# First attention of a two-layer gated cross-attention block: 64 unrolled slots, with probabilities and queries turned by VectorE and DMA

## The reference

```python
xn = layernorm(x);  q = xn @ Wq;  k = ctx @ Wk;  v = ctx @ Wv        # per head: 128 x 128
q = q * rsqrt(mean(q*q) + eps) * gq;  k = k * rsqrt(mean(k*k) + eps) * gk
p = softmax(q @ k.T / sqrt(128));  x = x + tanh(g_xattn[0]) * ((p @ v) @ Wo)
```

## Time and profile before

| What | Value |
|---|---|
| Median of 3 runs | 1292.04 us (1291.64 to 1292.76) |
| Profiled execution | 1293.64 us, span 1291.9 us, mean granted TensorE clock 0.992 |
| PE busy | 1238.0 us (96% of the span), 7907 matmuls |
| PEld busy | 1096.8 us (85%) |
| DVE busy | 893.5 us (69%), 2453 instructions |
| ACT busy | 737.3 us (57%), 2053 instructions |
| POOL busy | 550.6 us (43%), 542 instructions |
| DMA | 101.09 MB, mean 78 GB/s |

### The profile page before, as it was taken

One profiled execution on the slowest core, in us unless ns is written; L12 is line 12 of the kernel. 1 busy time (PEld: TensorE's weight loads), 2 busy tenths in 40 slices (PEclk: granted clock), 3 DMA queues, 4 the chain that ended last, 5 costly groups with the idle time before them and its releaser, 6 DMA issues. The chain is left out here.

```text
span 1291.9 us, 23370 instructions
## 1 busy us (share of the span) xinstructions
PE 1238.0 (96%) x7907; PEld 1096.8 (85%) x7907; DVE 893.5 (69%) x2453; ACT 737.3 (57%) x2053; POOL 550.6 (43%) x542
## 2 busy tenths in 40 slices
PE   6899999999999989999999989999999998999998
PEld 4788888888888878888888889898898987888987
DVE  6678788887988767743433235757777688788857
ACT  4877777777777744332222237766656554546542
POOL 4565456545566433200000001766667778223430
PEclk9999999999999989999999989999999999999999
DMA  8000000000000220299100000434334447413434
GB/s 268 10 1 1 9 1 1 1 9 0 0 0 1 65 41 2 64 331 293 65 0 1 1 18 17 152 120 123 115 107 142 124 126 251 119 46 101 131 100 174
DMA packets 85672, 101.09 MB, mean 78 GB/s; under 512 B 16985, under 2 KB 72802, under 8 KB 85186
## 3 DMA queue, kind: packets, MB, share of 16 engines
q1 hardware_dynamic: 82162, 90.45, 23.1%
q0 software_dynamic: 3408, 9.34, 2.0%
HBM read 53.60 MB, written 46.18 MB: 77 GB/s over the span
## 5 line engine op out<-in xcount | busy, mean ns | idle before, releaser
L98 PE MATMUL bank<-wvo_hi,pc_hi_a 128*128 128x256 f32 x512 | 148.8, 291 | 5.8 <-DVE pc_lo_a L1346 5.0
L1755 ACT ACTIVATE act_g_f<-bank 128x512 f32<-128x512 f32 x64 | 38.2, 598 | 191.1 <-PE bank L100 191.1
L100 PE MATMUL bank<-wvo_hi,pc_lo_a 128*128 128x256 f32 x512 | 143.8, 281 | 0.0
L99 PE MATMUL bank<-wvo_lo,pc_hi_a 128*128 128x256 f32 x512 | 143.7, 281 | 0.0
L1814 DVE TENSOR_TENSOR hid_f<-act_g_f,bank 128x512 f32<-128x512 f32 x64 | 44.0, 687 | 142.4 <-ACT act_g_f L1755 142.4
L883 ACT ACTIVATE probs_a<-bank,nbias_a,q_r_a 128x128 f32<-128x128 f32 x256 | 114.3, 472 | 23.6 <-DVE nbias_a L1001 23.4
L140 POOL TENSOR_TENSOR rstd<-mv,half 128x4 f32<-128x4 f32 x12 | 12.2, 1019 | 260.9 <-DVE mv L135 260.9
L1061 POOL TENSOR_TENSOR probs_a<-probs_a,rden_a 128x512 f32<-128x512 f32 x64 | 66.6, 1041 | 104.7 <-DVE rden_a L1007 104.7
L98 PEld LDWEIGHTS bank<-wvo_hi,pc_hi_a 128*128 128x128 f32 x512 | 97.4, 190 | 12.0 <-DVE pc_lo_a L1346 7.7
L1286 ACT ACTIVATE probs_a<-probs_a,nmin_a 128x128 f32<-128x128 f32 x256 | 99.6, 392 | 5.7 <-DVE nmin_a L1330 5.3
L98 PE MATMUL bank<-xt_hi_f,w_gu_hi_f 128*128 128x512 f32 (+1 forms) x256 | 101.2, 395 | 0.0
(11 more groups left out here) (314 smaller groups left out, 4138.7 us busy)
## 6 DMA issues: line engine op xcount, KB each, us to landing
rows_in<-blank_f SPq DMA_DIRECT2D x8, 2193.0 KB, 20.6
staged<-blocks_a SPq DMA_DIRECT2D x32, 512.0 KB, 2.9
turned_a<-staged SPq DMA_DIRECT2D x128, 128.0 KB, 3.0
xs_raw_f<-rows_in SPq DMA_DIRECT2D x39, 129.0 KB
y_tok_f<-rows_out SPq DMA_DIRECT2D x4, 1024.0 KB, 9.0
we_raw<-in_L_ffn_We_gate_up SPq DMA_DIRECT2D x2, 1408.0 KB, 9.6
ctx_raw_a<-in_ctx SPq DMA_DIRECT2D x8, 256.0 KB, 2.9
x_sb<-in_x SPq DMA_DIRECT2D x4, 512.0 KB, 9.9
```

The costliest lines, as they stand in the source:

```text
L98: nc.tensor.matmul(out, w[0], x[0], start=start, stop=False)
L99: nc.tensor.matmul(out, w[0], x[1], start=False, stop=False)
L100: return nc.tensor.matmul(out, w[1], x[0], start=False, stop=stop)
```

## The change

The first attention gets a function of its own, `first_attention`, and a flat order, `first_order`. The loop, the start, first, body and last parts and `quad_order` go. A slot v (from -7 to 71) holds one step of every kind, each for a unit that is some slots ahead or behind: for example Q of unit v+7, K of v+6, KT of v+3, S of v+2, EX of v+1, C of v-6 and W of v-7.

- T and QT leave TensorE. TV (VectorE) turns the probabilities of a unit in blocks, and TQ (VectorE) turns the queries straight out of the bank, in place of the copy Qv. SP swaps the blocks through DRAM for two units at a time, once for queries and once for probabilities. Qc (ScalarE) copies the landed queries, Th (ScalarE) the landed probabilities. Tl moves from VectorE to GpSimd.
- The powers of queries and keys become one GpSimd instruction for two units, RT, 16 values per row, once in two slots. Eps is added by a 129th column of the squares, so the two small VectorE additions go.
- The ring has three banks in place of two. `Kr` and `Qr` stay on VectorE, `KH` and `Rp` on GpSimd.
- The packed weights are loaded in parts: the first four tiles in slots 53 to 55, the scales in slot 57, the rest after slot 64. SC waits for the scales, CO of tile 0 for the first part and CO of tile 4 for the rest. The fed steps get new places by slot.

```diff
-FEED = {"Sm3": "SC0", "Tl1": "CO0", "Cl1": "LNB0", "Rp3": "VA0", "Tl3": "X0 X1", "Cl3": "CO1 VA1 DG0 DD0", "W0'": "CO2 VA2", "W1'": "DG1 DD1"}
+FEED = {55: "SC0", 56: "CO0", 57: "LNB0 VA0", 58: "X0 X1", 59: "CO1 VA1", 60: "DG0 DD0 CO2", 61: "VA2", 62: "DG1 DD1"}
...
+def first_order():
+    opening = """
+        WK0 CT0 CT1 LNA0 K0 Kc0 Kq0 K1 Kc1 Kr0 Kq1 LNB0 K2 Kc2 Kr1 Kq2 WQ0 K3 Kc3 Kr2 Kq3 X0 X1 Kr3 GN0"""
+    lead = {-7: "WK1", -6: "WQ1", -5: "VT0 VT1", -4: "VT2 VT3 CN0", -3: "VO0", -2: "WK2 VO1", -1: "WQ2 VO2", 0: "VO3", 1: "WK3 VO4", 2: "WQ3 VO5", 3: "VO6", 4: "VO7"}
+    norm = {0: "LA0", 1: "LA1", 2: "LA2", 3: "LA3", 4: "LM0", 5: "LB0", 6: "LB1", 7: "LB2", 8: "LB3 CT0", 10: "CT1"}
...
+    for v in range(-7, U + LAG):
+        s = v + 2 - LAG
+        if 0 <= v < U - H and v % H == 9:
+            words("X0 X1", v // H + 1)
+        unit(v + 2, "S")
+        unit(v + 6, "TQ", "Qq")
+        unit(v, "R", "Rp")
+        if v < U:
+            unit(v - 1, "TV")
+        unit(v + 3, "KT")
+        unit(v + 2, "Sm")
+        unit(v + 1, "EX")
+        unit(s, "C")
+        if v + 6 > 3:
+            unit(v + 6, "K")
+        if v + 5 > 3:
+            unit(v + 5, "Kr")
+        unit(v + 6, "Qr")
+        if v % 2 == 0:
+            unit(v + 4, "RT")
+        unit(v + 4, "KH")
+        words(lead.get(v, ""))
+        unit(s - 1, "W")
...
+        unit(s, "Ch", "Cl")
...
+        unit(v + 3, "KTc", "Qc")
+        if v + 6 > 3:
+            unit(v + 6, "Kc", "Kq")
+        unit(s + 1, "Th", "Tl")
+        unit(v + 7, "Q")
...
+            def swap(p, made, source, via, sent, target, landed, free, taken):
+                s = p % 2
+                sp.wait_ge(sem(made), 2 * p + 2)
+                if p >= 2:
+                    sp.wait_ge(sem(f"{landed}{s}"), 64 * (p // 2))
+                sp.dma_start(via[s], source[:, s, :, :, :].rearrange("p j u x -> p (j u x)")).then_inc(sem(sent), 16)
+                if p >= 2:
+                    sp.wait_ge(sem(free), taken)
+                sp.wait_ge(sem(sent), 16 * (p + 1))
+                rows = via[s].rearrange("(i r) (j x) -> j r i x", i=4, j=4)
+                for j in range(4):
+                    sp.dma_start(target[32 * j:32 * j + 32, s, :, :, :].rearrange("p i u x -> p i (u x)"), rows[j]).then_inc(sem(f"{landed}{s}"), 16)
...
+            for v in range(-5, U + 1):
+                if v % 2:
+                    p = (v + 5) // 2
+                    if p < U // 2:
+                        swap(p, "q_blocks_made", q_blocks, staged[1], "q_blocks_sent", q_turned, "q_landed", "q_copied", 2 * p - 2)
+                elif v >= 2:
+                    p = (v - 2) // 2
+                    swap(p, "blocks_made", blocks, staged[0], "blocks_sent", turned, "landed", "pt_ready", 2 * p - 2)
...
                 elif name == "KT":
+                    pe.wait_ge(sem("kh_ready"), n + 1)
...
+                elif name == "C":
...
+                    pe.wait_ge(sem("pt_ready"), n + 1)
+                    if n:
+                        pe.wait_ge(sem("pc_ready"), n)
...
+                elif name == "Qc":
+                    act.wait_ge(sem(f"q_landed{n // 2 % 2}"), 64 * (n // 4 + 1))
...
+                elif name == "TQ":
+                    dve.wait_ge(filled["Q"], n + 1)
...
+                    nc.vector.transpose(q_blocks[:, p % 2, :, n % 2, :].rearrange("p j (h t) -> p h j t", h=QH),
+                                        bank[:, :].rearrange("p (h j s) -> p h j s", h=QH, j=4)).then_inc(sem("q_blocks_made"), 1)
...
+                elif name in ("Kr", "Qr"):
...
+                    nc.vector.tensor_reduce(sums_of(kind, n), squares[:, n % 2, :, :], AX.X, ALU.add).then_inc(sem(f"{low}_summed"), 1)
...
+                elif name == "RT":
+                    pool.wait_ge(sem("q_summed"), n + 2)
+                    pool.wait_ge(sem("k_summed"), n + 2)
...
+                    nc.gpsimd.tensor_tensor(roots[:, p % 4, :, :, :].rearrange("p k u h -> p (k u h)"), ss[:, p % 2, :, :, :].rearrange("p k u h -> p (k u h)"),
+                                            core.half[:, :], ALU.pow).then_inc(sem("roots_ready"), 1)
                 elif name == "KH":
+                    pool.wait_ge(sem("roots_ready"), p + 1)
...
+                elif name == "Tl":
+                    pool.wait_ge(sem("pt_hi_ready"), n + 1)
+                    hi, lo = (v[:, n % 2, :].rearrange("p (i x) -> p i x", i=4) for v in pt)
+                    nc.gpsimd.tensor_tensor(lo, turned[:, n // 2 % 2, :, n % 2, :], f32(hi), ALU.subtract).then_inc(sem("pt_ready"), 1)
```

More of the change, by code:

```diff
@@ L441 @@
 PREPARE = ("UV", "UK", "UC", "UO", "UQ", "UM", "MB")
[L442 to L480, removed]
@@ L483, in with_weights @@
[L483 to L495, removed]
+FIRST_RING = ("X", "CT", "K", "Q", "KT", "VT", "VO")
+RING = ("X", "Q", "SR", "NX", "RT", "RK", "XF")
+DRAINED = {"Qc": "Q", "RL": "RT", "PL": "RK"}
@@ L496, in attention, with first_attention @@
+def first_attention(nc, core, block, w, a, norm, norm_after, packed, feed):
     ctx_dram = a["ctx_1024"]
@@ L522, in attention @@
[L522 to L533, removed]
-            q_r = sb("q_r", [P, 2, GB, QH])
-        else:
-            cm = sb("cm", [P, GB, P])
-            scores = probs
@@ L588, in walk @@
-        def walk(emit):
-            if L == 0:
-                for s in orders["start"]:
-                    emit("start", -1, *s)
-                for s in orders["first"]:
-                    emit("first", 0, *s)
-                with emit.engine.Fori(1, G - 1) as g:
-                    for s in orders["body"]:
-                        emit("body", g, *s)
-                for s in orders["last"]:
-                    emit("last", G - 1, *s)
-            else:
-                for g, *s in flat_order:
-                    emit("flat", g, *s)
@@ L663, in _ @@
+            for t in range(4, NF0 // P, 4):
+                for m in range(3):
+                    packed.load_words(sp, m, t)
+            feed.rest["sync"](sp)
         @block.tensor
         def _(pe):
[L665 to L685 removed]
@@ L687, in _, with bank_free @@
-            fed = feed.steps["tensor"](pe) if feed else None
-            def step(part, g, name, i, j):
-                m = round_of(name, g, j)
+            fed = feed.steps["tensor"](pe)
+            def bank_free(step):
+                at = ring.index(step)
+                if at >= 3:
+                    old = ring[at - 3]
+                    pe.wait_ge(sem({"Q": "q_squared", "K": "k_copied", "KT": "kt_copied", "X": "x_split", "CT": "ct_split", "VT": "vt_copied",
+                                    "VO": "vo_split"}[old[0]]), count(*old))
+                return ring_bank[at % 3]
@@ L907, in _ @@
+                    if n:
+                        act.wait_ge(sem("c_filled"), n * H)
+                    nc.scalar.activation(flat(cn[0][:, :, :]), flat(ctx_raw[:, :, :]), ACT.Copy).then_inc(sem("cn_hi_ready"), 1)
+            feed.rest["scalar"](act)
         @block.vector
         def _(dve):
-            fed = feed.steps["vector"](dve) if feed else None
-            def step(part, g, name, i, j):
-                m = round_of(name, g, j)
+            fed = feed.steps["vector"](dve)
+            for name, n, i in order:
+                bank = bank_of(name, n, i)
+                p = n // 2
@@ L1036, in _ @@
-            if feed:
-                feed.rest["vector"](dve)
+            feed.rest["vector"](dve)
         @block.gpsimd
         def _(pool):
-            fed = feed.steps["gpsimd"](pool) if feed else None
-            def step(part, g, name, i, j):
-                m = round_of(name, g, j)
+            fed = feed.steps["gpsimd"](pool)
+            nc.gpsimd.memset(core.ident[:, :], 0.0).then_inc(sem("zeroed"), 1)
+            nc.gpsimd.memset(core.half[:, :], -0.5).then_inc(sem("half_made"), 1)
@@ L1433, in flamingo @@
                     with nc.Block() as block:
-                        attention(nc, core, block, layer, w, a, gate_up, norm, norm_ffn, packed, router, None, feed)
+                        first_attention(nc, core, block, w, a, norm, norm_ffn, packed, feed)
                 else:
```

736 lines of the change are left out of this document (285 added, 451 removed).

## The result

The changed kernel takes 1305.8 us (median of 4 runs, 1303.74 to 1306.29); the kernel before took 1292.4 beside it. The ratio is 1.0098, 95% interval 1.0081 to 1.0116: 13 us slower, where 28 us faster was forecast. The profiled execution took 1305.93 us, its span is 1304.2.

The account below looks back on a forecast made before the run. A two-slot chain through in-order queues, 12.7 us a pair, bounds the first attention; 75 + 317.5 + 2 roots + 27 + 29, plus 2 for the clock, puts the first product at 453 instead of 480.57: 1264 us, range 1234 to 1286.

Parts of the forecast that it names:

- The chain of a plain pair: First attention, two slots: closed loop from Q through TQ, Kr, RT, KH, Tl, C, K, W to Q, 12.7 us.
- Then 25 pairs (slots 6 to 55) x 12.7 = 317.5, plus two layer norm roots of 1.0: Middle of the first attention: every pair at chain length, two 1.0 us roots before Tl in slots 20 and 36.
- the refills: Turning tokens and context (X0, X1, CT0, CT1) ahead of each later group; the prediction's sum gave them no term.
- the 0.39: TensorE time per unit before the change, in us: short waits and the turns of `xn` and `ctx`.
- Slot 6 starts at about 75: Opening of the first attention: first Q at 19 us, slots -7 to -3 some 14, then four times some 10.5.
- Four times 10.5: Slots -2 to 5, without C and W: pair's chain ends at KT, with two weight products some 10.5 us, four times 42.
- Slots 61 to 70 ... 2.9 each: Tail: C, Ch, Cl and W through single `c_bank` 2.2 to 2.4 us, with fed steps 2.9 each, 29 us.
- Slots 56 to 60 ... some 27: Start of the tail: slots still have RT or KH but lose Q and K, some 27 us.
- rival 1: First attention: TensorE sets the pace, VectorE early; 5.7 us a unit, 32 less, 1232 us; chance 0.14.
- rival 2: First attention: same chain but longer, VectorE late or GpSimd slower; 13.4 us a pair, 1282 us; chance 0.19.
- rival 3: First attention: SP's swap queue sets the pace; at twice today's write wait 15.1 us a pair, 1324 us; chance 0.07.
- The rule on memory at high load: Swap writes to DRAM: estimated 1.8 us more per write, SP held 13.2 us a pair, time 12 us longer.

Follow-up runs that it names:

- experiment 7: Changed kernel with only the ring's order altered: VO, CT0, X0, CT1 ahead of KT, X1 ahead of K; 1291.65 us, ratio 0.9992 to the kernel before.
- experiment 5: Changed kernel without turning tokens and context (X0, X1, CT0, CT1) for groups 2 to 4; 1289.37 us, ratio 0.9979 to the kernel before.
- Experiment 8: Changed kernel with VO1 to VO7, WK2, WK3 and WQ2 left out of the opening, WQ3 moved to slot 37; 1299.55 us.
- experiment 2: Changed kernel with only Th moved to the start of the slot, Tl staying behind RT and KH; 1301.81 us.
- experiment 4: Changed kernel with Th and Tl first in the slot and the root replaced by an addition of -0.5; 1260.54 us.
- experiment 12: Changed kernel with Th and Tl first, Kr early and the ring reordered, plus Rp behind KH and TV behind Qr; 1248.73 us.

## Why the prediction was wrong

**The chain of a plain pair was right.** 12.8 us instead of 12.7, with the two waits of TensorE in the place and order given, RT at 2.90, and GpSimd back to back from RT to Tl. Two smaller points: TQ from a bank took 0.64 from start to start where 0.60 was put in, and the lower bound of 12.0 was added wrongly (12.7 less 0.81 and 0.60 is 11.3).

**What failed is how the chain was carried over the span.** The prediction had the first product at 453; it stands at 492.96. The 40 us have three places.

- "Then 25 pairs (slots 6 to 55) x 12.7 = 317.5, plus two layer norm roots of 1.0": from the TQ of slot 6 (87.33) to that of slot 56 (429.04) it is 341.7, 22.2 more than 319.5. Plain pairs are 25 x 12.81 = 320; the rest is three times 7.1, and only the roots of it had been counted. The sum put the refills at nothing. I had read the ring of three banks as one bank more than before and did not ask which fill each Q and KT follows there once an item comes in between. Of the 7.1 a group, 1 is the root and 3.9 go when only the order of the items changes (experiment 7); without the items 5.5 go (experiment 5). The other 2.2 hold the items' own work on TensorE, which stood in the 0.39 that the 12.7 left out; how much it is, no run shows. This step would alone have taken the gain from 27.5 to 5.
- "Slot 6 starts at about 75": 87.33. "Four times 10.5" was TensorE's chain alone; ScalarE's copies of the weights, in order ahead of KTc, which frees Q's bank, were not in it. Experiment 8 shows 8.8 of the 12.3; of the other 3.5, 1.75 is a first Q at 20.75 us instead of 19; for the rest no run was made (the granted clock of 20 to 40 and 40 to 60 us is 0.90 and 0.91, in the kernel before 0.95 and 1.00).
- The tail: from the TQ of slot 56 on it is 63.9 us instead of 56 + 2, and both of its terms were short. "Slots 61 to 70 ... 2.9 each": 3.5, from the C of slot 61 (460.69) 32.3 us instead of 29. I took the loop through `c_bank` and overlooked the one through Th behind Ch; with Th first (experiment 2) a slot takes 3.2. "Slots 56 to 60 ... some 27": from C (430.13) to C 30.6. In them S waits 2.10 us for a late Qc, and behind that wait the granted clock of 440 to 450 us is 0.69, between its two levels (a pass of C took 0.63 in it where 0.39 is usual), the kind of gap for which 2 us had been added. With Th first the whole tail is 61.7, with Th and Tl first 60.4, and 57.9 without the root as well.

The sum is 12.3 + 22.2 + 5.9 = 40.4. The prediction said that the ends rest on the fewest rows; the larger error was in the middle, which it held to be the firm part.

**The rivals.** TensorE did not set the pace (rival 1), but it nearly does so once the order is mended: 5.54 us a slot in experiment 4, 5.54 and 5.65 in experiment 12. The longer chain (rival 2) did not come in plain pairs: 12.8, not 13.4. Over all 25 pairs the mean is 341.7 / 25 = 13.7, near the 13.8 at which rival 2 saw no gain, but by slots with refills and not by a chain that is longer in every pair. SP's queue (rival 3) is not it: two doubled writes a pair were needed to bring it near. Slower came by a mechanism that none of the three named.

**The rule on memory at high load.** The writes of the swaps were waited for 46.4 / 15 = 3.1 and 44.8 / 15 = 3.0 us at 155 GB/s, after 2.73 at 120 GB/s: 0.3 to 0.4 more. From issue to landing the page of the profile has 3.3 and 3.4 us for them and 2.9 for those of the kernel before. By the 2 us at high load of the Trainium skill, "DMA: Bandwidth & Descriptors", section "Latency and other measured facts", I had estimated 1.8 more. The trace shows 0.3 to 0.5 more at this load, and the measurement decides; a higher load was not run.

## What to carry to other kernels

When work is moved off the busiest engine, the new pace is a loop through in-order queues. Look for the second-longest loop as well as the longest: here 12.8 and 12.05 us a pair stood beside one another; the root left out alone gave 9 us, Th and Tl first alone 18, both 45. A step whose input has long been there (Th, Tl) belongs at the front of its engine's slot, not behind steps that wait. Around a ring of buffers, write down for every slot that has an extra item which fill each fill has to follow.
